# A two-layer graph attention kernel: first-stage logits from raw rows of x, and layers that gather raw rows of x

## The reference

```
xn  = layernorm(x)                                # mean and deviation of each row
# layer 1: 4 heads of 512
h   = (xn @ W1).reshape(N, 4, 512)
as_n, ad_n = sum(h * a1_src), sum(h * a1_dst)     # per node and head: "logits"
e   = leaky_relu(as_n[src] + ad_n[dst], 0.2)
alpha = softmax of e over the edges with one dst
h1  = elu(segment_sum(alpha * h[src], dst) + b1)  # 2048 wide
# layer 2: the same with one head, W2, 768 wide; out + b2
x1  = x + layer2
out = x1 + ffn(layernorm(x1))                     # 96 hidden
```

## Time and profile before

| | |
|---|---|
| median of three runs | 4165.0 us |
| the profiled execution | 4167.93 us, its span 4166.2 us |
| granted TensorE clock, mean | 0.939 |
| TensorE busy | 3571.3 us, 86% |
| VectorE busy | 2228.8 us, 53% |
| ScalarE busy | 1354.7 us, 33% |
| GpSimd busy | 850.1 us, 20% |
| HBM read, written | 266.01 MB, 124.25 MB |

### The profile page before, as it was taken

The page is one execution under the profiler, slowest core; times in us unless marked ns, Lnnn a source line. Parts: engine busy times, 40 slices in busy tenths (PEclk is TensorE's granted clock), DMA queues, the critical chain, the costliest instruction groups (busy, mean ns, idle before and its releaser), DMA issues. The chain is left out here.

```text
span 4166.2 us, 68773 instructions
## 1 busy us (share of the span) xinstructions
PE 3571.3 (86%) x22440; PEld 2183.9 (52%) x22441; DVE 2228.8 (53%) x5433; ACT 1354.7 (33%) x2327; POOL 850.1 (20%) x1236
## 2 busy tenths in 40 slices
PE   4860019999999999999999999999999996388888
PEld 3640015565556556655655565566556654256565
DVE  8877345334434443443344344434443434699998
ACT  2531104323322332333233223323332333244444
POOL 2448720000000000100000000000000100266665
PEclk9985559999999999999999999999999998699999
DMA  8862011111111111111111111121111100378887
GB/s 256 256 213 83 3 27 41 55 40 46 39 58 36 45 42 54 41 39 48 39 51 38 55 37 43 42 60 36 42 45 40 53 27 15 84 207 231 233 236 209
DMA packets 142471, 337.79 MB, mean 81 GB/s; under 512 B 76839, under 2 KB 76917, under 8 KB 134775
## 3 DMA queue, kind: packets, MB, share of 16 engines
q1 hardware_dynamic: 111976, 240.96, 19.0%
q0 software_dynamic: 29056, 92.87, 8.6%
q10 hardware_dynamic: 1175, 0.05, 0.0%
HBM read 266.01 MB, written 124.25 MB: 94 GB/s over the span
## 5 line engine op out<-in xcount | busy, mean ns | idle before, releaser
L1394 PE MATMUL lay_pm<-lay_zh,w1h 128*128 128x500 f16 x1920 | 718.9, 374 | 26.0 <-DVE lay_h L1280 19.6
L1117 POOL DMA_INDIRECT lay_rows<-parts,lay_idx x200 | 209.7, 1048 | 2536.7 <-PE lay_pz L1360 1616.3
L1395 PE MATMUL lay_pm<-lay_zl,w1h 128*128 128x500 f16 x1920 | 719.2, 375 | 3.2 <-issue 3.1
L1396 PE MATMUL lay_pm<-lay_zh,w1l 128*128 128x500 f16 x1920 | 718.9, 374 | 0.0
L1201 DVE SCALAR_TENSOR_TENSOR lay_zl<-lay_pz,lay_zh 128x400 f16<-128x400 f32 x600 | 319.5, 573 | 708.3 <-ACT lay_zh L1311 708.3
L1311 ACT ACTIVATE lay_zh<-lay_pz 128x400 f16<-128x400 f32 x600 | 297.9, 503 | 1054.2 <-PE lay_pz L1360 1050.2
L1320 ACT ACTIVATE lay_ex<-lay_pm,b1c,scale 128x500 f32<-128x500 f32 x320 | 245.5, 767 | 873.7 <-PE lay_pm L1396 873.7
L1418 PE MATMUL lay_pm<-w2h,lay_gh 128*128 128x512 f16 x1280 | 485.0, 379 | 0.0
L1418 PE MATMUL lay_pm<-w2h,lay_gl 128*128 128x512 f16 x1280 | 483.9, 378 | 0.0
L1418 PE MATMUL lay_pm<-w2l,lay_gh 128*128 128x512 f16 x1280 | 483.4, 378 | 0.0
L1236 DVE TENSOR_SCALAR lay_ex<-lay_ex,scale 128x500 f32<-128x500 f32 x320 | 153.6, 480 | 571.8 <-ACT lay_ex L1320 571.8
(11 more groups left out here) (308 smaller groups left out, 5600.6 us busy)
## 6 DMA issues: line engine op xcount, KB each, us to landing
x<-in_x_dram SPq DMA_DIRECT2D x20, 1500.0 KB
out_x<-x SPq DMA_DIRECT2D x100, 288.0 KB
out_own<-h SPq DMA_DIRECT2D x100, 288.0 KB
out_dram<-out_x SPq DMA_DIRECT2D x100, 288.0 KB
nrm_xb<-in_x_dram SPq DMA_DIRECT2D x20, 1344.0 KB
parts<-nrm_parts SPq DMA_DIRECT2D x20, 1344.0 KB
h<-lay_h SPq DMA_DIRECT2D x80, 336.0 KB
nrm_w<-in_L_gnn_W_dram SPq DMA_DIRECT2D x6, 1024.0 KB, 19.6
```

What stands on the lines that cost most here:

```text
L1394: pe.matmul(o, c.w1h[:, d, cols], zh[:, d, h], start=(d == 0), stop=False)
L1395: pe.matmul(o, c.w1h[:, d, cols], zl[:, d, h], start=False, stop=False)
L1396: ins = pe.matmul(o, c.w1l[:, d, cols], zh[:, d, h], start=False, stop=(d == DC - 1))
```

## The change

The first stage (`stage_logits`) no longer writes normalised rows. It turns raw rows of x, without waiting for their statistics, and multiplies `v1` with all 500 turned rows of a block at once: `v1` is held, six multiplications of 500 columns per block. As the dot product with a normalised row is (dot with the raw row, less mean times the sum of the vector) times the inverse deviation, `finish` on VectorE corrects the logits afterwards, with `vsum` from one small multiplication. The stage stores a table of ten numbers per node: 8 logits, mean, inverse deviation. The softmax stage gathers those ten (40 bytes instead of 32) and puts mean and deviation into the records, now 16 numbers instead of 12. The layer stage gathers raw rows of x (3072 bytes, as before); ScalarE makes the high half (`high_rows`), VectorE normalises in place and takes the rest (`low_rows`, into the same bytes) before TensorE uses them. One more transfer per strip fetches mean and deviation of the strip's nodes. The buffer `h2` is single instead of double.

```diff
-    turned_logits, xb, parts, logit (four buffers each), pb (two)
+    x, table (four buffers), lines (two), pd (one), pv, vsum
 (VectorE, first stage)
+            def finish(s, b, j):
+                q = Chain(dve, table_chain, s)
+                dve.wait_ge(rstd_ready, s + 1)
...
+                q.put(nc.vector.tensor_tensor(shift[:], mean broadcast, vsum broadcast, ALU.mult))
+                nc.vector.tensor_copy(table[:, b, :, 2 * HEADS], mv[:, b, :, 0])
+                nc.vector.tensor_copy(table[:, b, :, 2 * HEADS + 1], rstd[:, b])
+                q.wait()
                 dve.wait_ge(turned_back, s + 1)
+                nc.vector.tensor_tensor(shift[:], pd[:], shift[:], ALU.subtract).then_inc(shifted, 1)
+                dve.wait_ge(shifted, s + 1)
+                nc.vector.scalar_tensor_tensor(out=table[:, b, :, 0:2 * HEADS], in0=shift[:], scalar=1.0 / SX,
...
             def step(s, b, j):
-                for t in range(NT):
-                    nc.vector.tensor_scalar(xb[:, b, t], xb[:, b, t], mv[:, b, t, 0:1], rstd[:, b, t:t + 1], ALU.subtract,
-                                            ALU.mult).then_inc(xs_ready, 1)
                 if within(s + 1):
                     statistics(s + 1, (b + 1) % NB, j + (b + 1) // NB)
-                for t in VECTOR_LOWS:
...
+                    copy_lines(s - 1, (b - 1) % NB)
+                if within(s - 2):
+                    finish(s - 2, (b - 2) % NB, j - (b < 2))
                 if within(s + 1):
                     refine(s + 1, (b + 1) % NB)
 (the statistics and refine of block 0 now stand behind the 48 reductions)
 (TensorE, first stage)
+            def dots(s, b):
+                pe.wait_ge(xt_ready, NT * s + NT)
+                if within(s, 2):
+                    pe.wait_ge(lines_ready, s - 1)
                 for k in range(DC):
+                    ins = pe.matmul(pl[b % 2][:], v1[:, k], xt[:, b % 2, k], start=(k == 0), stop=(k == DC - 1))
+            def lines_there(s):
+                pe.wait_ge(lines_ready, s + 1)
+                if within(s, 1):
+                    pe.wait_ge(shifted, s)
             def step(s, b, j):
                 for t in range(NT):
+                    if t == 2 and within(s, 1):
+                        lines_there(s - 1)
+                    turn(s, b, t, j)
...
+                    if t == 0 and within(s, 1):
+                        dots(s - 1, (b - 1) % NB)
+                    if t == 2 and within(s, 1):
+                        turn_back(s - 1, (b - 1) % NB)
 (layer stage)
+EARLY_ROWS = {8: 0, 10: 1}
+                sp.dma_start(slots[WE:128, :, 11:13],
+                             dr.logit1[bass.ds(SN * q, SN), 2 * HEADS:TW1].rearrange("(i p) w -> p i w", p=WN),
...
+            def low_rows(rc, q, i):
+                at = raw[:, i % 2]
+                dve.wait_ge(hi_done, WPS * q + i + 1)
+                rc.link(nc.vector.tensor_scalar(at, at, mean[:, i:i + 1], scale[:, i:i + 1], ALU.subtract, ALU.mult))
+                nc.vector.tensor_tensor(rows_lo[:, i % 2, 0:D], at, rows_hi[:, i % 2], ALU.subtract).then_inc(lo_done, 1)
...
+            def high_rows(q, i):
...
+                act.wait_ge(gathered[i % 2], 16 * (WPS // 2) * q + 16 * (i // 2 + 1))
+                nc.scalar.activation(rows_hi[:, i % 2], raw[:, i % 2], ACT.Identity, bias=bias[:, i:i + 1],
+                                     scale=scale[:, i:i + 1]).then_inc(hi_done, 1)
...
             def window(q, i, first):
-                pe.wait_ge(gathered[i % 2], 16 * (WPS // 2) * q + 16 * (i // 2 + 1))
+                pe.wait_ge(hi_done, WPS * q + i + 1)
+                pe.wait_ge(lo_done, WPS * q + i + 1)
```

More of the change, by code:

```diff
@@ L51 @@
 XE = 64
-REC = 12
+REC = 16
 MAX_CHUNKS = E // XE + 1
@@ L370, in copy_turned @@
[L370 to L378 removed]
+                    copy_turned(s, b, t)
@@ L1325, in body @@
                         high(s, k - 1)
+                    if k in EARLY_ROWS and not last:
+                        high_rows(s + 1, EARLY_ROWS[k])
                 high(s, KC - 1)
```

271 lines of the change are left out of this document (139 added, 132 removed).

## The result

The changed kernel takes **4132.8 us** (median of four runs, 4131.2 to 4133.7) beside 4162.9 for the kernel before on the same chip (4158.7 to 4170.4): ratio 0.9929, 95% interval 0.9915 to 0.9943. That is 30 us faster. I had forecast 4155 with a range of 4136 to 4182: the sign of the likeliest case was right, the gain was three times as large, and the time lies outside the range.

What follows compares the result with a forecast made beforehand. TensorE was taken to bound the strips, VectorE's chain the first stage's blocks. First stage -32, softmax stages +1.6, fill +20 and strips 0 gave -10 us on the 4165 median: 4155 us, range 4136 to 4182.

Steps and rivals of the forecast that it cites:

- the likeliest case: Whole kernel: the forecast itself, 10 us faster at 4155 us, within 4147 to 4163, chance 0.4.
- First stage, block time: First stage: VectorE stops being the bound, and a block takes 10.15 us instead of 12, waits of 0.9 and 0.35 included.
- The lower bound of -36: First stage: the largest gain allowed around its -32 us, with no loop work and W1 early.
- Logits: First stage: six products by 500 columns take 5.1 us a block, against 5.5 for 24 by 125.
- the rule that I had set against it: First stage: next weights load while columns stream, so the swap saves nothing, logits stay 5.5 us, total 4163.
- Start and end: First stage: weight vectors at 45 us, TensorE released at 63, block 1's logits done at 72, stage end at 257.
- Softmax stages: Both softmax stages: wider gathered rows, two copies and a larger record store cost +1.6 us, bounds 0 and +4.
- Fill: Layer stage's first ten windows: row operations lengthen the window chain, +20 us, bounds +10 and +27.
- Rival 2: Fill costs +10 instead of +20 because window chains overlap or cold products partly limited it; total 4143, chance 0.25.
- rival 1: First stage: TensorE's clock falls in the new waits, 27 us lost, total 4182, chance 0.12.
- Strips: Layer stage's 190 later windows: added ScalarE and VectorE work (+158 and +304 us) stays hidden, 0 us.
- The added transfer for the slots: Ahead of the fill: transfer of 500 pieces of 8 bytes, between 0 and 5 us, taken as 2.4.

Runs made afterwards that it cites:

- experiment 1: Changed kernel with the three independent small VectorE operations of `finish` each made to wait for the one before; 0.9950 of the kernel before, first stage 258.3 us.
- experiment 3: Changed kernel with two PSUM banks for the turned-back logits instead of one; 0.9909 of the kernel before, first stage 239.9 us.
- experiment 6: Changed kernel plus unread multiplications in the fill, 30 before window 0 and 12 before each later even window; 0.9923 of the kernel before, fill 82.4 us.
- experiment 10: Changed kernel with experiment 5's order and unread products in the fill, 14 before each even window, 8 behind the last; 0.9897 of the kernel before, fill 75.2 us.
- experiment 5: Changed kernel with, in the fill alone, an odd window's high and low parts ahead of the next even window's rows; 0.9912 of the kernel before, fill 79.4 us.
- experiment 7: Changed kernel with the first operation of `low_rows` done twice for every window; 0.9928 of the kernel before, strips 2835.5 us.
- experiment 9: Changed kernel with 432 tiny unread multiplications in TensorE's program ahead of the layer stage's first wait; 0.9934 of the kernel before, strips 2836.5 us.
- experiment 12: Kernel before with 432 tiny unread multiplications in TensorE's program ahead of the layer stage's first wait; 0.9974 of the kernel before, strips 2830.7 us.
- experiment 4: Changed kernel with VectorE's line copies of blocks 0 and 1 placed earlier; 0.9924 of the kernel before, first stage 245.4 us.

## Why the prediction was wrong, point by point

**First stage, block time: the failing step.** "VectorE does the line copy (0.66) and the first four ops of `finish` (about 0.8) after the logits end, 0.2 for drain and hand-over, 1.7 us in all": copy, operations and hand-over are 1.2 to 1.4 us, because four small operations that don't wait for each other cost 0.1 each, not 0.2. The wait is 0.50 to 0.58 us in the loop and 0.36 behind it, instead of 0.9; ScalarE's is 0.25 to 0.33 instead of 0.35. The 0.1 for the loop's register work was there, inside these waits: a block in the loop takes 0.17 to 0.25 us more than one behind it, with the same work. That the loads of x had ended by then is not the reason: block 3, ahead of the loop with the loads running, took 9.47 us. A block took 9.53 us on average instead of 10.15: 11.1 us over 18 blocks. With 2 us from an earlier start and 1.3 from the stage's end that is the 14.4 us of the first row. Experiments 1 and 3 show this term from both sides. The same trace that I read for the earlier trace rows held both prices. Unlinked operations, three in 0.30 us, and a linked one, 0.19 behind the L301 of the earlier trace rows:

```profile
269.82 0.30 DVE L293 BATCH_NORM_AGGREGATE nrm_mv<-nrm_stats 125x2 f32<-125x12 f32 x3
...
274.75 0.17 DVE L302 TENSOR_TENSOR nrm_sq<-nrm_sq,nrm_ve 125x4 f32<-125x4 f32 x1
```

I took the 0.16 us of L301 and rounded it up to a spacing. The lower bound of -36 had the same error in it, so the range was too narrow on that side.
The Trainium skill (Perfetto Trace Analysis, Optimizing Scalar/DVE Operations) says of the overhead that each VectorE instruction has that the profiled latency is about twice the time for which the engine is busy, since the second half overlaps with the next instruction. The rows of these small operations agree, 0.15 us long and 0.07 apart.

**Logits.** Six products by 500 columns in 5.1 us: right (5.13). That the old form would cost 5.5 was wrong (5.22 in the same place), and it didn't enter the sum; the rule that I had set against it was right that the swap saves nothing, and the 4163 us I had drawn from it were wrong, since they kept the 5.5.

**Start and end.** First reduction at 12.4 us instead of 15.5 (I had bounded it by 13.5), weight vectors 41.8 us instead of 45, TensorE's release 59.6 instead of 63, the logits of block 1 finished at 70.0 instead of 72: the order of events and their chain were right, W1 came earlier.

**Softmax stages.** +1.6 forecast for both together, -0.4 measured for the first; the second lies in the last row of the table and can't be told from its spread. No run shows a cost of the wider records.

**Fill.** +20 forecast, +23.4 measured: right in mechanism and near in size, the latter in part by luck. Up to the first window it was +3.6 (forecast 5.6), over the four pairs +16.4 (12.5), behind them +3.4 (2): two terms too small and one too large. ScalarE's row operation takes 1.03 us, not the 0.83 of L364; low rows took the 1.6 us forecast. What I had left out is the clock: longer waits put nearly all products of the fill at the lower level, 1.5 us in each window, of which 0.9 and 1.0 us a pair came back when TensorE was kept busy (experiment 6 against the changed kernel, 10 against 5). Rival 2 (a fill that costs less) was wrong, and rival 1's mechanism was right in a place where I had not looked for it. The added transfer for the slots cost about 0.5 us (near's memset to the indices, 9.28 to 9.83 us), where I took 2.4.

**Strips.** "So 0" was right for what I argued about: 158 and 304 us of added work are hidden (the strips took no longer), and 129 more are as well (experiment 7). The 8.5 us came from something that no term of mine covered, the place of TensorE's loop in its code (experiments 9 and 12): 5.70 to 5.14 us a pass. That is a fourth of the profiled gain, and has nothing to do with what the change computes. Its size is less sure than its cause: the same padding moved the strips by 4.0 us in the changed kernel and by 10.3 in the kernel before.

**The total.** -46.4 - 0.4 + 23.4 - 8.5 - 2.7 = -34.6 us in the two profiled executions, -30 in the medians: the profiled one of before lay 5 us above its median. Neither miss alone would have left the range (4155 - 14 = 4141, 4155 - 8.5 = 4146.5); together they did. The 2.7 us at the end stay open; variants of one code spread there by several us (673.7 to 683.7).

## What to carry to other kernels

Read the distance between the starts of small operations, not their durations, and ask whether they wait for each other: linked ones cost 0.20 us each here and unlinked ones 0.07 to 0.10, and where they stand between an engine's result and the wait for it, this is multiplied by every block. Where a change makes waits longer, check the granted clock of that stretch, and where it removes one, follow the queue to the next semaphore (experiment 4) before counting the gain. And when a loop becomes faster for no reason in its own code, compare the code pieces fetched per pass: here padding ahead of a loop was worth 11 us in one kernel and cost 4 in another.

## What the runs showed of the hardware that I had not expected

- 432 useless products outside a loop of 18 passes made a kernel 11 us faster, as the loop came to fetch 2 pieces of code per pass instead of 10; in the changed kernel the same padding went the other way and cost about 4 us.
- The 3000 columns of a block's float32 logits take 5.13 us in 6 products and 5.22 in 24.
- Doubling one VectorE operation per window raised GpSimd's mean time for a gather in the strips from 1051 to 1097 ns (190 gathers each), and the strips' time does not show it.
